# A new order of work for the first routed feed-forward of a Flamingo block

## The reference, cut to what matters

```python
def feed_forward(x, gamma, w1, b1, w2, b2):
    h = jax.nn.gelu(rms_norm(x, gamma) @ w1 + b1, approximate=False)
    return h @ w2 + b2
light_out = feed_forward(x, light_gamma, light_w1, ...)       # hidden width 128, all tokens
s = jnp.einsum('bnd,d->bn', x, routing_token)
scores = coor_descent(s, 256 * 9 / 8, 50, 1.0)                 # 50 serial logsumexp steps over 1024
sel_scores, sel_idx = jax.lax.top_k(scores, 256)
# heavy_out: feed_forward with hidden width 1024 for the 256 chosen tokens of each sequence
```

## Time and profile before

| | us |
|---|---|
| median of 3 runs (lowest, highest) | 3290.38 (3288.73, 3294.31) |
| the profiled execution's own time | 3289.11 |
| its span, first to last instruction | 3287.4 |
| stage `l0f`: first DMA issue to first one of `l1x` | 157.7 to 331.8 |

### The profile page before, as it was taken

How to read it: one execution, slowest core, us unless ns; L and a number is a source line. 1 busy time by engine, 2 the same in 40 slices (tenths; PEclk the granted TensorE clock), 3 DMA queues, 4 the chain that set the end, 5 groups by cost and what they waited for, 6 DMA issues and landing times. The chain is left out here.

```text
span 3287.4 us, 41337 instructions
## 1 busy us (share of the span) xinstructions
PE 2956.4 (90%) x15957; PEld 1581.2 (48%) x15973; DVE 1659.4 (50%) x3305; ACT 1291.2 (39%) x1784; POOL 1299.5 (40%) x1038
## 2 busy tenths in 40 slices
PE   7889899999999999686889999978888899998798
PEld 3456334434434344244458889843333223322587
DVE  4535555564455455466662112147553877776400
ACT  4432444344343434346521111124333465565232
POOL 2241366565666556610235222214555210000433
PEclk9999999999999999897999999989998999999899
DMA  1400100000000000000006455520001000000376
GB/s 54 123 17 1 38 6 5 11 5 6 5 10 6 5 6 1 26 0 28 1 30 235 168 214 199 209 83 6 1 14 36 1 1 1 1 1 1 123 242 173
DMA packets 72758, 172.03 MB, mean 52 GB/s; under 512 B 17501, under 2 KB 52242, under 8 KB 59764
## 3 DMA queue, kind: packets, MB, share of 16 engines
q0 software_dynamic: 21744, 118.63, 10.5%
q1 hardware_dynamic: 50820, 50.75, 4.9%
HBM read 142.23 MB, written 27.64 MB: 52 GB/s over the span
## 5 line engine op out<-in xcount | busy, mean ns | idle before, releaser
L1520 POOL TENSOR_TENSOR l1x_added<-l1x_added,l1x_probs 128x1024 f32<-128x1024 f32 x224 | 527.2, 2354 | 264.9 <-ACT l1x_probs L1791 198.6
L1888 DVE TENSOR_REDUCE l1x_tops<-l1x_ring 128x1 f32<-128x512 f32 x512 | 326.8, 686 | 192.9 <-PE l1x_ring L1600 192.6
L1121 DVE TENSOR_REDUCE l3a_halves<-l3a_ring 128x1 f32<-128x512 f32 x512 | 325.0, 684 | 99.6 <-PE l3a_ring L966 95.4
L1791 ACT ACTIVATE l1x_probs<-l1x_slots 128x1024 f32<-128x1024 f32 x256 | 261.7, 1024 | 238.9 <-PE l1x_slots L1644 237.1
L1637 PE MATMUL l1x_slots<-l1x_Q,l1x_K 64*128 64x512 f32 x1152 | 309.5, 615 | 6.0 <-ACT l1x_probs L1789 4.8
L1082 ACT ACTIVATE l3a_probs<-l3a_slots 128x1024 f32<-128x1024 f32 x256 | 248.2, 1021 | 160.6 <-PE l3a_slots L986 160.6
L1659 PE MATMUL l1x_pv<-l1x_probs,l1x_V 128*64 128x512 f32 x1152 | 284.4, 610 | 0.0
L986 PE MATMUL l3a_slots<-l3a_Q,l3a_K 32*128 32x512 f32 x1024 | 150.2, 637 | 35.5 <-ACT l3a_probs L1082 34.7
L3439 DVE TENSOR_TENSOR l2f_hh<-l2f_sg,l2f_hid 128x256 f32<-128x256 f32 (+1 forms) x184 | 69.9, 381 | 214.2 <-ACT l2f_sg L3286 214.2
L3286 ACT ACTIVATE l2f_sg<-l2f_hid 128x256 f32<-128x256 f32 (+1 forms) x184 | 64.5, 351 | 282.6 <-PE l2f_hid L3202 280.4
L3202 PE MATMUL l2f_hid<-l2f_xgT,l2f_gate 128*128 128x256 f32 (+1 forms) x736 | 167.7, 351 | 3.1 <-ACT l2f_xgT L3273 2.4
(11 more groups left out here) (706 smaller groups left out, 5192.8 us busy)
## 6 DMA issues: line engine op xcount, KB each, us to landing
l1x_w<-in_l_qkv SPq DMA_DIRECT2D x16, 384.0 KB, 3.1
slots_in<-zeros SPq DMA_DIRECT2D x1, 4992.0 KB, 18.2
l2f_yg<-rows_out SPq DMA_DIRECT2D x8, 512.0 KB, 5.6
l2f_xg<-slots_in SPq DMA_DIRECT2D x15, 272.0 KB, 3.6
slots_in<-zeros SPq DMA_DIRECT2D x1, 2944.0 KB, 19.3
x<-in_x SPq DMA_DIRECT2D x4, 512.0 KB, 7.9
l1f_w<-in_l_w SPq DMA_DIRECT2D x2, 1024.0 KB, 7.0
x<-x SPq DMA_DIRECT2D x4, 512.0 KB, 2.9
```

What stands on the lines that cost most here:

```text
L1121: nc.vector.tensor_reduce(halves[:, k % 2, col:col + 1], bank_of(banks[e]), AX.X, ALU.max).then_inc(s["bank_done"], 1)
L1520: ins = nc.gpsimd.tensor_tensor(added[h][:], added[h][:], probs[:, n % PROBS, :, :], ALU.add)
L1791: ins = nc.scalar.activation(p, s2[m % 2], ACT.Exp)
L1888: ins = nc.vector.tensor_reduce(tops[:, e * NT + t, h:h + 1], bank, AX.X, ALU.max)
```

## The change

Seven edits, all inside `plan0` and `ffn0`:

1. The statistics of all four chunks come first on VectorE. GpSimd's `norm` makes only `size` and `lean`; `ratio` of all chunks is made at once later (`rates`), and the scores in one operation in `find_best`.
2. ScalarE scales `w1l` and VectorE `w1h`. The DMA of `w1h` is issued ahead of that of `b1`.
3. TensorE runs 24 and 8 matmuls of constants (`busy`) around the first transposes; ScalarE loads the gelu table at its start.
4. GpSimd adds the light bias to `x` after the exponentials of centre 0 rather than in the head.
5. 16 pieces stand ahead of round 0, where 20 stood.
6. One piece stands after every round, where one and two alternated; two pieces between `final` and `rows`, where four stood.
7. `out` is taken and biased in two halves of 128x512, not at once.

```diff
-    plan = [("norm", 0), ("norm", 1), ("turn", 0), ("dot", 0)]
+    plan = [("stats", n) for n in range(NC)]
+    plan += [("norm", 0), ("busy", 24), ("norm", 1), ("turn", 0), ("dot", 0), ("busy", 8)]
...
-    work(3)
-    plan.extend([("norm", 2), ("turn", 1), ("dot", 1)])
+    plan.append(("norm", 2))
+    work(2)
+    plan += [("norm", 3), ("turn", 1), ("rates",)]
+    work(2)
+    plan += [("dot", 1), ("dot", 2), ("dot", 3), ("turn", 2)]
     work(4)
-    plan.extend([("norm", 3), ("turn", 2), ("dot", 2)])
-    work(4)
-    plan.extend([("turn", 3), ("dot", 3)])
-    work(3)
+    plan.append(("turn", 3))
+    work(2)
     plan.append(("best",))
...
-            work(1 + i % 2)
+            work(1)
     plan.append(("final",))
-    work(4)
+    work(2)
     plan.append(("rows",))
...
-                step.add(pool.tensor_scalar(ratio[:, n, :], var, EPS, None, ALU.add))
...
+            def rates():
+                step.add(pool.tensor_scalar(ratio[:], mv[:, :, :, 1], EPS, None, ALU.add))
+                step.add(pool.tensor_tensor(floor[:], floor[:], size[:], ALU.mult))
                 step.wait()
-                pool.tensor_tensor(ratio[:, n, :], ratio[:, n, :], floor[:, n, :], ALU.mult).then_inc(s["size_ready"], 1)
...
+                step.add(pool.tensor_tensor(ratio[:], ratio[:], down[:], ALU.pow))
+                step.wait()
+                pool.tensor_tensor(ratio[:], ratio[:], floor[:], ALU.mult).then_inc(s["ratio_ready"], 1)
...
+            def add_biases():
+                pool.wait_ge(s["xn_ready"], NC)
+                pool.wait_ge(s["ex_ready"], 1)
...
-            def heavy(n):
-                chunk = yh[:, n * CT:(n + 1) * CT, :]
-                pool.wait_ge(s["heavy_kept"], n + 1)
-                pool.tensor_tensor(chunk, chunk, b2h[:].unsqueeze(1).broadcast_to([P, CT, D]), ALU.add).then_inc(s["heavy_added"], 1)
+            def heavy(n, i):
+                part = yh[:, n * CT + 2 * i:n * CT + 2 * i + 2, :]
+                pool.wait_ge(s["heavy_kept"], 2 * n + i + 1)
+                pool.tensor_tensor(part, part, b2h[:].unsqueeze(1).broadcast_to([P, 2, D]), ALU.add).then_inc(s["heavy_added"], 1)
...
+            def keep_busy(n):
+                for _ in range(n):
+                    nc.tensor.matmul(hid[:, 1, 0:P], c.ident[:], c.ones[:], start=True, stop=True)
...
+            def scale_light():
+                act.wait_ge(s["gam_loaded"], 16)
+                act.wait_ge(s["w1l_loaded"], 16)
+                for k in range(KD):
+                    nc.scalar.activation(w1l[:, k, :], w1l[:, k, :], ACT.Copy, scale=gam[:, k, 0:1]).then_inc(s["w1l_scaled"], 1)
...
+            nc.scalar.preload_act_table_set("gelu_and_others")
...
+            def scale_heavy():
+                dve.wait_ge(s["gam_loaded"], 16)
+                dve.wait_ge(s["w1h_loaded"], 16)
+                for k in range(KD):
+                    nc.vector.tensor_scalar(w1h[:, k, :], w1h[:, k, :], gam[:, k, 1:2], None, ALU.mult).then_inc(s["w1h_scaled"], 1)
```

More of the change, by code:

```diff
@@ L2096, in _ @@
             sp.dma_start(tok[:], row_tile(io["l0_token"], P)).then_inc(s["tok_loaded"], 16)
-            sp.dma_start(w1l[:], io["l0_w1l"].rearrange("(k p) m -> p k m", p=P)).then_inc(s["w1_loaded"], 16)
+            sp.dma_start(w1l[:], io["l0_w1l"].rearrange("(k p) m -> p k m", p=P)).then_inc(s["w1l_loaded"], 16)
+            sp.dma_start(w1h[:], io["l0_w1h"].rearrange("(k p) m -> p k m", p=P)).then_inc(s["w1h_loaded"], 16)
             sp.dma_start(b1[:], io["l0_b1"]).then_inc(s["b1_loaded"], 16)
-            sp.dma_start(w1h[:], io["l0_w1h"].rearrange("(k p) m -> p k m", p=P)).then_inc(s["w1_loaded"], 16)
             sp.dma_start(w2l[:], io["l0_w2l"]).then_inc(s["w2_loaded"], 16)
@@ L2166, in _ @@
                     norm(e[1])
-                    if e[1] == 1:
-                        scale_weights()
-                elif e[0] == "dot" and e[1] == 3:
+                elif e[0] == "rates":
+                    rates()
                     set_rest()
+                elif e[0] == "centre" and e[1] == 0:
+                    add_biases()
                 elif e[0] == "light":
                     light(e[1])
-                elif e[0] == "heavy" and e[2:] == (CT - 1, MH - 2):
-                    heavy(e[1])
+                elif e[0] == "heavy" and e[2] % 2 and e[3] == MH - 2:
+                    heavy(e[1], e[2] // 2)
                 elif e[0] == "centre" and e[1]:
@@ L2193, in hidden @@
                     if n == 0 and i == 0:
-                        pe.wait_ge(s["w1_scaled"], 4)
+                        pe.wait_ge(s["w1l_scaled"], KD)
+                    if n == 0 and i == 1:
+                        pe.wait_ge(s["w1h_scaled"], KD)
                     if i == 0:
@@ L2220, in heavy @@
                     last = nc.tensor.matmul(out[:, t, :], hh[:, k + j, t * P:(t + 1) * P], w2h[:, k + j, :], start=k + j == 0, stop=k + j == MH - 1)
-                if t == CT - 1 and k == MH - 2:
+                if t % 2 and k == MH - 2:
                     last.then_inc(s["heavy_psum"], 1)
@@ L2246, in _ @@
             for e in plan:
-                if e[0] == "turn":
+                if e[0] == "busy":
+                    keep_busy(e[1])
+                elif e[0] == "turn":
                     turn(e[1])
@@ L2291, in light, with heavy @@
                                      scale=gate_col).then_inc(s["light_kept"], 1)
-            def heavy(n):
-                act.wait_ge(s["heavy_psum"], n + 1)
-                nc.scalar.activation(yh[:, n * CT:(n + 1) * CT, :].rearrange("p t d -> p (t d)"), out[:].rearrange("p t d -> p (t d)"), ACT.Copy,
+            def heavy(n, i):
+                act.wait_ge(s["heavy_psum"], 2 * n + i + 1)
+                part = yh[:, n * CT + 2 * i:n * CT + 2 * i + 2, :]
+                nc.scalar.activation(part.rearrange("p t d -> p (t d)"), out[:, 2 * i:2 * i + 2, :].rearrange("p t d -> p (t d)"), ACT.Copy,
                                      scale=gate_col).then_inc(s["heavy_kept"], 1)
@@ L2456, in _ @@
                     dot(e[1])
+                    if e[1] == 0:
+                        scale_heavy()
                 elif e[0] == "best":
```

39 lines of the change are left out of this document (16 added, 23 removed).

## The result

The changed kernel takes 3272.33 us (median of five runs, 3269.76 to 3280.05) against 3292.39 before (five runs, the three above among them, 3288.73 to 3294.58): ratio 0.9946, 95% interval 0.9930 to 0.9961, that is 17.8 us less (12.8 to 23.0). The prediction said 3274. The profiled execution took 3269.76, its span is 3268.0, against 3287.4 before: 19.4 shorter. Not all of that is the change's, so the parts are taken apart here.

A forecast was written before the change was run, and what follows sets the result against it. TensorE bounds the stage from round 0 on, behind a head in which it mostly waits; 19.1 - 3.45 - 3.7 + 4.0 = 16.0 us off 3289.11 gives 3273.1, said as 3274 for the median, range 3269 to 3282.

The forecast's parts named there:

- head: From the start of stage `l0f` to round 0: round 0 comes at 185.6 instead of 204.73, 19.1 us gained.
- pieces moved behind round 0, and stalls: From round 0 on: four pieces moved behind it cost 3.45 us, TensorE's waits at the centres and `final` 3.7.
- The rounds: The 49 routing rounds: one piece behind each gives 1.09 us, TensorE's own time, so they cost TensorE nothing more.
- the 0.14 of slack: In a one-piece round, TensorE's 1.09 us less the 0.95 of the chain through VectorE.
- the bound rounds: Rival: the 49 rounds become bound by their chain, 0.16 us lost in each, 8 in all, 3281; chance 0.09.
- the additions that hold them up: Rival: GpSimd's bias additions delay VectorE's operations in the rounds, 5.4 + about 5 us lost, 3284; chance 0.05.
- The centres: Steps between rounds at worse places: TensorE loses 0.7 and 1.35 us at centre 1, 1.4 at centre 2.
- that bound: Round 0, with both operands in SBUF, may be held up by GpSimd's additions: taken as 0, can be 0.4 us.
- The tail: From TensorE's last piece to the stage's last tile: 2.86 us instead of 6.89, 4.0 gained.
- The rival's chance of 0.02: Rival: a stall in centre 1 lowers the clock and the rounds don't restore it, up to 3298; chance 0.02.

The follow-up runs named there:

- the first execution: The changed kernel's first profiled execution, unedited, with a fall of the clock just behind centre 1; its stage `l0f` lasted 159.71 us.
- the second one of the changed kernel: The changed kernel run again unedited, for a second profiled execution; stage 158.06 us, ratio 0.9956 to the kernel before.
- one filled wait: The kernel before with twelve useless 128x128 matmuls in TensorE's 3.17 us wait for the best scores; round 0 at 47.05 us, stage 174.16, ratio 0.9993.
- the best place: The changed kernel with other numbers of pieces behind the rounds, which moves the centres to their places in the kernel before; stage 156.68 us, ratio 0.9937.

## Why the prediction was right

| step | predicted | measured |
|---|---|---|
| head | 19.1 | 47.01 - 27.72 = 19.3 |
| pieces moved behind round 0, and stalls | -3.45 - 3.7 = -7.15 | round 0 to last copy, 126.24 - 119.12 = -7.1; in the first execution -8.8 |
| ScalarE's last copy to the next stage | 4.0 | 7.97 - 4.08 = 3.9 |
| stage | 16.0 | 174.10 - 158.06 = 16.0; in the first execution 14.4 |

The measured column sets the one profiled execution of the kernel before against the second one of the changed kernel; neither has a fall of the clock from the transpose of the best scores on.

**The head** came out as laid out. The first hidden matmul started at 9.80 after the stage's start (predicted 10.0). Some operations were mis-sized without effect: the power over 16 columns takes 3.20, not up to 5.8, the scaling of `w1l` 0.34 each, not 0.3, and the dots 0.42, not 0.52. VectorE's scalings of `w1h`, which were to shut GpSimd out for 1.4, ran beside a power of GpSimd that took 1.55 instead of 1.04, and nothing waited for it.

**The rounds** keep their 1.08; the 0.14 of slack is enough (the 0.25 for wait and weight load in it has no row; just behind centre 1 TensorE's matmul starts 0.06 after the reduction's end, so the slack is rather larger), and VectorE's reductions are at 0.17 beside GpSimd's additions. Two rivals fall with that, the bound rounds and the additions that hold them up. **The centres**: 0.57 and 1.15 waited at centre 1, where 0.7 and 1.35 were said, and 1.28 at centre 2, where it was 1.4. Round 0, which the prediction named as the one that the additions could hold up, took its 0.17 and had started 0.06 ahead of them, so that bound was not tried.

**The tail**: 0.69 + 1.26 + 0.88 and hand-overs, 2.97 against 2.86. The halved copy was sized at 0.60 and takes 0.69. VectorE waited 18.22 ahead of the last chunk's first half, as said ("some 20").

**What was not right** is how the clock was treated, in both directions. The rival's chance of 0.02 was for a clock that falls and stays down; it fell in one execution of eight, and came back after two rounds, for 1.7. The argument against it, full clock over the earlier trace rows, was of a stretch without waits, and said nothing of one with them. And the base was a lucky execution: the 3.17 us wait ahead of the best scores, which the change removes, costs the kernel before another 2.6 in most executions. The prediction did not count that gain, and its 16.0 is therefore below the estimated 17.8. Its 3274 lies 1.7 from the measured 3272.33; runs of one kernel differ by 10, so that nearness is luck, while the 16.0 of the stage is not. The profiled difference of 19.4 holds 5.4 from the program's start, which the change doesn't touch, and too little from a stage in which the clock fell.

**The edits weighed.** The short spacing was taken as a gain, since it takes the counting out of the end. It does that, but at the old head it is worth nothing without the halves, and with the new head it loses 1.6 against the old spacing.

## What to carry to other kernels

When the sought difference is under what two runs of the same kernel differ by, compare the stretch that the change touches, and compare the granted clock in it first. Where two chains meet at an end, test each edit alone and both together. A serial step that borrows an engine should be put where nothing soon waits for that engine: in the best place the centres cost TensorE nothing, in the changed kernel 0.58 + 1.15 + 1.30 = 3.0 us of waiting.

## What the runs showed of the hardware

- Behind short waits of TensorE its clock was sometimes at 1.2 instead of 2.4 GHz for a few us, and with the same code in some executions only: behind 0.57 + 1.15 us of waiting in one of eight, behind 3.17 in three of four, behind 2.39 in its one execution, not behind the two of 1.04 and 1.05 in theirs. That the waits are the cause is supported by one filled wait (3.17) and not proved.
- The program's first matmuls of 512 columns took 3.78 for four in eleven of fourteen profiled executions and 1.98 in three, though the granted clock reads 1.00 from 18 to 30 us in all. `l0f` then started 157.6 to 159.4 us into the program instead of 152.0 to 152.3. The five that started at 159.0 or later also have a granted clock of 0.96 between 60 and 100 us, where all others have 1.00. Nothing that differs between these kernels comes ahead of `l0f`.
- Beside GpSimd's additions over 128x1024, VectorE's operations on two columns with all inputs in SBUF took 1.31 to 2.27 instead of 0.16 to 0.22 us; those of the rounds, with an input in PSUM or a reduction, kept their 0.17.
- GpSimd's power costs 0.73 for 2 columns, 1.04 for 4 and 3.20 for 16.
